# Expert numbers read four at a time, W2 loads in the order of free buffers, and part of the result stored from ScalarE

## What is computed

```python
logits = x2 @ Wr + br
expert = jnp.argmax(softmax(logits), axis=-1)        # one of 8 experts for each node
h   = gelu(einsum('ecd,edf->ecf', buf, W1) + b1)     # W1: 8 x 512 x 128
out = einsum('ecf,efd->ecd', h, W2) + b2             # W2: 8 x 128 x 512
y   = out[slot] * gate
# shared = gelu(x2 @ Ws1 + bs1) @ Ws2 + bs2
# result = x + shared + bank_sp(x) + bank_fq(x)
```

## Time and profile before

| What | Value |
|---|---|
| Runs | 533.3, 534.15, 535.89 us; median 534.15 |
| The profiled execution, time | 538.39 us |
| Its span from first to last instruction | 536.6 us |
| Mean granted TensorE clock | 0.966 |
| PE busy | 476.1 us, 89% of the span |
| DVE, ACT, POOL busy | 224.5, 166.2, 191.8 us |
| SPq's share of the chain that ended last | 11% |

### The profile page before, as it was taken

How to read it: one execution, slowest core, us unless ns; L and a number is a source line. 1 busy time by engine, 2 the same in 40 slices (tenths; PEclk the granted TensorE clock), 3 DMA queues, 4 the chain that set the end, 5 groups by cost and what they waited for, 6 DMA issues and landing times.

```text
span 536.6 us, 7670 instructions
## 1 busy us (share of the span) xinstructions
PE 476.1 (89%) x2638; PEld 328.7 (61%) x2638; DVE 224.5 (42%) x561; ACT 166.2 (31%) x363; POOL 191.8 (36%) x201
## 2 busy tenths in 40 slices
PE   2798999979999997989999999999999999997390
PEld 2344457767566654766677778777877777564050
DVE  4789953213444456432220024300266955353026
ACT  2799663212211117212130133400544232121000
POOL 2103000190502511980537533060362688230072
PEclk9999999989999998999999999999999999999586
DMA  5999999958999789658027001200230037888875
GB/s 120 407 424 420 423 385 347 373 190 296 393 408 414 265 308 413 244 172 333 5 58 217 0 1 4 98 4 1 59 99 0 1 96 220 240 253 243 272 218 167
DMA packets 36597, 115.30 MB, mean 215 GB/s; under 512 B 6495, under 2 KB 6556, under 8 KB 28110
## 3 DMA queue, kind: packets, MB, share of 16 engines
q1 hardware_dynamic: 34318, 112.22, 58.3%
q0 software_dynamic: 2240, 2.57, 1.8%
HBM read 105.76 MB, written 9.01 MB: 214 GB/s over the span
## 4 chain that ended last, share of the span: by engine, by line
PE 64%; SPq 11%; DMA 10%; issue 8%; POOL 3%; DVE 2%; ACT 2%; DVEq 0%; POOLq 0%
PE ps L1494 13%; PE ps L1496 12%; PE ps L1495 12%; PE ps L1853 9%; PE ps L1518 9%; DMA ring<-in_L_gnn_basis_dram 8%; SPq L576 5%; SPq L577 4%; PE ps L1579 2%; PE ps L1698 2%; DMA got<-y_dram,slot_u 1%; PE ps L1502 1%; POOL piece_lo L670 1%; PE ps L1756 1%; ACT h_tmp L1254 1%
## 5 line engine op out<-in xcount | busy, mean ns | idle before, releaser
L1518 PE MATMUL ps<-ring,sel_att 128*32 128x512 f32 x512 | 67.8, 617 | 6.2 <-DMA ring<-in_L_gnn_basis_dram 2.7
L1494 PE MATMUL ps<-piece_hi,ht_hi 128*125 128x512 f32 x140 | 56.1, 401 | 0.8 <-PE ps L1496 0.6
L1495 PE MATMUL ps<-piece_lo,ht_hi 128*125 128x512 f32 x140 | 55.1, 394 | 0.0
L1496 PE MATMUL ps<-piece_hi,ht_lo 128*125 128x512 f32 x140 | 55.1, 394 | 0.0
L1001 DVE SCALAR_TENSOR_TENSOR u_lo<-ps,gates,u_hi 125x512 fp32r<-125x512 f32 x20 | 15.0, 751 | 94.1 <-ACT u_hi L1402 94.1
L669 POOL CAST piece_hi<-piece_raw 128x512 fp32r<-128x512 f32 x28 | 19.9, 710 | 95.1 <-issue 70.7
L670 POOL TENSOR_TENSOR piece_lo<-piece_raw,piece_hi 128x512 fp32r<-128x512 f32 x28 | 37.5, 1339 | 14.4 <-issue 12.3
L851 DVE TENSOR_SCALAR oh_n<-iota_n,keys 125x626 f16<-125x626 f16 x100 | 38.1, 381 | 8.3 <-PE ps L1579 6.2
L1853 PE MATMUL ps<-u_hi,cf 125*125 125x512 f32 x100 | 39.9, 399 | 1.3 <-PE ps L1496 1.3
L1853 PE MATMUL ps<-u_lo,cf 125*125 125x512 f32 x100 | 39.4, 394 | 0.0
L732 POOL TENSOR_SCALAR sort<-iota_s,slot_s 125x864 fp32r<-125x864 f32 x10 | 24.4, 2447 | 32.0 <-PE ps L1941 21.1
(11 more groups left out here) (323 smaller groups left out, 959.9 us busy)
## 6 DMA issues: line engine op xcount, KB each, us to landing
ring<-in_L_gnn_basis_dram SPq DMA_DIRECT2D x64, 1024.0 KB, 9.4
w_home<-in_L_ffn_W_sp_dram SPq DMA_DIRECT2D x27, 256.0 KB, 2.9
w_home<-in_L_ffn_W_fq_dram SPq DMA_DIRECT2D x24, 256.0 KB, 3.1
rel_dram<-stag SPq DMA_DIRECT2D x16, 256.0 KB, 8.4
w_raw<-rel_dram SPq DMA_DIRECT2D x8, 512.0 KB, 6.7
piece_raw<-in_L_mix_Wkqv_dram SPq DMA_DIRECT2D x3, 1024.0 KB, 10.6
y_dram<-ybuf SPq DMA_DIRECT2D x12, 256.0 KB, 3.7
piece_raw<-in_L_mix_W_dram SPq DMA_DIRECT2D x2, 1024.0 KB, 10.8
```

What stands on the lines that cost most here:

```text
L1494: pe.matmul(target, a_hi, b_hi, start=first, stop=False, skip_group_check=skip)
L1495: pe.matmul(target, a_hi, b_lo, start=False, stop=False, skip_group_check=skip)
L1496: return pe.matmul(target, a_lo, b_hi, start=False, stop=last, skip_group_check=skip)
L1518: last = pe.matmul(ps[32 * c:32 * c + 32, rel_bank(ch), :], sel_att[:, ch // CHUNKS, g].rearrange("p r q -> p (r q)"), ring[slot][:, c * D ...
```

## The change

Four edits, all in the last stage.

1. The units are numbered in another order: the last four W1 units of the second bank become 12 to 15, Ws1 becomes 16 and Ws2 17. ACT's and POOL's order follow from that, and POOL's two Ws units no longer stand between its sort tiles.
2. SP begins its W2 loads after unit 12; units 13 to 16 are loaded behind the first three W2 tiles, and unit 17 behind tiles 3 and 13.
3. SP reads the numbers of a tile's blocks with one instruction, four (or three) at a time; tiles are loaded in another order against the stores of finished tiles.
4. Rows 112 to 124 of each result tile are stored from ACT's queue.

```diff
-        UNITS = ([(1, 0, e) for e in range(E)] + [(1, 1, e) for e in range(4)] + [(1, 2, 0), (2, 2, 0)] +
-                 [(1, 1, e) for e in range(4, E)])
+        UNITS = ([(1, 0, e) for e in range(E)] + [(1, 1, e) for e in range(E)] + [(1, 2, 0), (2, 2, 0)])
...
-            for n in range(RAWS, len(UNITS)):
+            for n in range(RAWS, UNIT[1, 1, 4] + 1):
                 load_unit(n)
...
-                for c in range(y_rows(j) // SB):
-                    at = b * NB + 4 * i + c
-                    expert = sp.value_load(block_ei[0:1, at:at + 1], min_val=0, max_val=E - 1)
+                at, count = b * NB + 4 * i, y_rows(j) // SB
+                _, experts = nc.values_load_multi_w_load_instructions(
+                    block_ei[0:1, at:at + count], engines=[mybir.EngineType.SP], min_val=0, max_val=E - 1)
+                for c, expert in enumerate(experts):
                     sp.dma_start(w2_home[HOME[j]][:, c, :], w2_of[b][bass.ds(expert, 1), :, :].rearrange("e f n -> f (e n)")
                                  ).then_inc(w2_in[HOME[j]], 16)
-            for j in (0, 1, 2, 3, 2 * NY - 1):
+            for j in range(3):
                 load_w2(j)
-            for j in range(2 * NY):
-                if j < 3:
-                    load_w2(j + 4)
-                elif j == 3:
-                    for i in range(NY, NY + 3):
-                        load_w2(i)
-                elif j < NY:
-                    load_w2(j + 6)
+            for n in range(UNIT[1, 1, 4] + 1, len(UNITS) - 1):
+                load_unit(n)
+            load_w2(3)
+            load_w2(2 * NY - 1)
+            load_unit(len(UNITS) - 1)
+            load_w2(4)
+            load_w2(5)
+            store_block(0)
+            load_w2(6)
+            store_block(1)
+            for j in range(NY, 2 * NY - 1):
+                load_w2(j)
+                if j > NY:
+                    store_block(j - NY + 1)
+            for j in range(NY, 2 * NY):
                 store_block(j)
             for t in range(NT):
                 sp.wait_ge(final_ready, t + 1)
-                for a, b in ROWS:
-                    sp.dma_start(out[t * TP + a:t * TP + b, :], x1[a:b, t, :]).then_inc(stored, 16)
+                a, b = ROWS[0]
+                sp.dma_start(out[t * TP + a:t * TP + b, :], x1[a:b, t, :]).then_inc(stored, 16)
...
-            unit_rest(UNIT[1, 1, 0], UNIT[1, 2, 0])
+            unit_rest(UNIT[1, 1, 0], UNIT[1, 1, 4])
...
             for t in range(P_TURNS, NT):
                 sort_tile(0, t)
-                unit_rest(UNIT[1, 2, 0] + t - P_TURNS, UNIT[1, 2, 0] + t - P_TURNS + 1)
             unit_rest(UNIT[1, 1, 4], len(UNITS))
...
             shared_row(1)
+            for t in range(NT):
+                act.wait_ge(final_ready, t + 1)
+                a, b = ROWS[1]
+                act.dma_start(out[t * TP + a:t * TP + b, :], x1[a:b, t, :]).then_inc(stored, 16)
```

## The result

The changed kernel takes 526.74 us (median of 4 runs, 526.35 to 527.45) against 535.02 for the one before (4 runs, 533.3 to 537.32): ratio 0.9844, 95% interval 0.9802 to 0.9886. It is 8.3 us faster, half of the 16.7 that was forecast, and the time lies above the range.

The account below looks back on a forecast made before the run. SP's queue of W2 loads and stores was taken to set the last 95 us. Tile 6's store 15.8 us earlier plus 0.9 from the last stores made 16.7: 534.15 - 16.7 = 517.5 us, range 515 to 523.5.

Parts of the forecast that it names:

- The start and the order: SP's loads: first read at 425.8, brief wait before unit 17, about 8 us before tile 4; PE's tile 0 0.94 earlier.
- I take 0.30, since it is one instruction on adjacent words of one row: SP's read of four numbers costs 0.30 us, a group 3.50 instead of 4.40; 40 reads fewer, 12.0 us of SP's work.
- The bounds, one read and four: SP's read of four costs no less than one read, 0.27 us, and not well more than four, 4 x 0.27.
- by the register: Rival: SP's read of four costs by the register, group up to 4.30 us, end 519.5 to 524.4; chance 0.21.
- The 0.6 us that the sum had for reads behind waits: On SP from tile 4 on: a read right after a wait takes up to 0.56 instead of 0.27.
- A store's landing: Tile 6's store, issued at 490.2, lands in about 3.58 us as before, so the first gather starts at 494.1.
- the DMA engines become the bound: Rival: late W2 loads and stores need 329 GB/s against 302, nine rounds 3.2 us longer, end 520.7; chance 0.12.
- The other chain: PE's second-bank tiles end at 496.1, 16.6 us earlier; the second gather keeps its distance to the first.
- ACT's work on Ws2: Rounding Ws1 and Ws2 costs ACT about 1.1 us more, hidden in 3.79 us of idle time; put at nothing.
- The range checks: On SP, 0.27 us per block kept; if cheap within a group, SP gains up to 3 us, about 1.2 arriving.
- the stall for unit 17: Rival: SP waits long for POOL's low half before unit 17, end 545, 11 us later than now; slower, chance 0.03.
- a gain lost behind POOL: Rival: gain lost behind PE or POOL, only 0.94 and 0.9 us remain, end about 532; chance 0.04.

Follow-up runs that it names:

- the probes: The changed kernel with range-checked idle reads of varied start and count added on SP, in its wait before tile 4 and behind five stores; 536.38 us including them.
- Experiments 2 and 3: 2: the changed kernel with one read per block again, 529.22 us. 3: the kernel before with the grouped reads alone, old order and stores, 529.41 us.
- the aligned kernel: The changed kernel with one word of padding, so the second bank's numbers start at word 28 instead of 27; 519.38 us, again side by side 521.04.
- 7: The kernel with padded numbers, reading four words for the two tiles of three blocks too (fourth unused, DVE clears the row first); 521.01 us, repeated 522.14.

## Why the prediction was wrong

**The start and the order were right.** SP's first load stands 2.1 us after `block_ei` (0.2 for the write, then the read and eight checks of the whole group), the wait for unit 17 is 1.3 us and harmless, SP stands 8.4 us ahead of tile 4 (about 8 forecast), the 0.94 of idle time before PE's first sort is gone, and PE's tile 0 starts 452.18 - 423.52 = 28.7 us after `block_ei`; before, 455.41 - 425.57 = 29.8.

**The step that failed is "I take 0.30, since it is one instruction on adjacent words of one row".** It is right for the six groups of four of the first bank and wrong for the six of the second, which stand in the stretch that sets the end, and for both groups of three. The bounds, one read and four, had the 0.87 of a word-by-word read inside them, and the rival "by the register" named it; what neither had is that the price depends on the start address, and that such a read can grow to 1.65 us, beyond the upper bound of 1.07. So the 526.7 lies above that rival's 524.4 too. Tiles 7 to 12 cost 7.7 us in reads instead of 1.8, tile 6 0.4 more: together 6.3 us. Tile 6's store is 6.0 us later than in the sum, counted from `block_ei` (494.13 - 423.52 = 70.6 instead of 490.2 - 425.57 = 64.6). With one word of padding it is at 489.64 - 424.72 = 64.9. The 0.6 us that the sum had for reads behind waits rests on a wrong reading of the earlier trace rows: the 0.56 stands 1.58 us behind a store, and in the changed kernel the reads of tiles 4 and 5, behind waits for PE, took 0.30 and 0.29.

The sentence on the Trainium skill's rule ("Runtime: NRT & Kernel Launch", section "Instruction fetch mechanics", about 200 ns for each register even in bulk) comes out as follows: 0.20 for each further word is what the probes show for every read but the aligned four, and there the rule doesn't hold.

**A store's landing was mis-sized:** 3.58 taken, 4.96 measured, which makes the gather start another 1.4 us later. The sum took the time of a store behind evenly spaced loads and used it for one behind four loads in a burst. Experiments 2 and 3 show that the grouping goes with it and the mean traffic doesn't. An estimate from rows gives about half of the size: four loads, 1.0 MB, issued within 2.0 us, against engines that moved at most 379 to 400 GB/s here, leave about 0.3 MB ahead of the store, some 0.7 us. Where the rest comes from is open. The rival "the DMA engines become the bound" had its ceiling at 302 GB/s, which is wrong, since 379 were moved; in the changed kernel it didn't come (share 0.80), in the aligned one it begins (0.97).

**The rest:** from the first gather to the end of DVE's adds it took 499.43 to 521.06 = 21.6 us, 0.45 less than before; the last stores brought 0.7 in the profile (0.9 forecast), which the runs can't show. Sum: 6.0 + 1.4 - 0.45 + 0.2 = 7.2 us, what was to be found in the stage.

**The other chain** was forecast too early as well, without harm. PE ended its tiles 78.7 us after `block_ei` (502.26), where the sum had 496.1 - 425.57 = 70.5. It waited for loads which SP issued late, and behind the first wait the granted clock was 0.50 (1.2 GHz) from 494.41 to 504.65, and 1.00 (2.4 GHz) until then: tile 12 took 1.94 us and tile 13 1.93, where the sum had 0.96 and 0.72 at full clock (columns as in the earlier trace rows). The earlier trace rows already had 1.93 for tile 13 before. POOL then waited 0.92 us for the second bank's stores, where it had waited 0.77 before. ACT's work on Ws2, which the sum put at nothing, cost nothing: ACT waited 2.67 us for Ws2 and PE's tile 0 did not wait. That hangs on the grouped reads, since with single ones (experiment 2) PE waited 1.0.

```profile
494.50:504.60 10.10, 5.97 (x23) 2.99 (x24) 1.82 (x4) 0.60 (x1) 4.26 (x4) 0.50 0.90 269
```

**The range checks** stayed near their full price in a group, 0.15 + 0.02 with their gaps, 0.26 for each number (1.02 for four, 491.04 to 492.06, instead of 1.08); the reservation that they could get cheap was not needed. Without them the first gather starts 5.8 us sooner, counted from `block_ei` (64.3 instead of 70.1 in 7), and the runs show nothing of it.

**The other rivals:** the stall for unit 17 and a gain lost behind POOL did not come. With the reads as forecast, in the aligned kernel, the stage is 96.4 us where the forecast had 111.0 - 16.7 = 94.3. What lacks there is the landing of the stores: tile 6's is issued within 0.3 us of the forecast, and the gather starts 6.2 us behind it instead of 3.9.

**Left open:** what it is in a store's issue that lengthens a read 1 to 2 us later, and whether an aligned four is spared because it is one piece or because it was nearly always over by then. The one that wasn't took 0.44. An experiment that puts aligned fours 1.6 us behind the stores would tell; none was made.

## What to carry to other kernels

When one instruction takes the place of several, its price is not between one and four by guess: measure it at each address and count that the loop will use, above all at those where the second half of a table begins. A queue that only issues (SP here) can be the bound of a stage, so count its reads, checks and issues like arithmetic. And where an edit bunches transfers that were evenly spaced, count on the one at the end of the bunch to land later: part of the queue's gain is paid back there.

## What was not expected of the hardware

- SP reads four words into registers in 0.30 us if the first stands at a multiple of four words, and in 0.87 if not; one word costs 0.27, two 0.47, three 0.67, at the starts tried (0 and 1, for two words 2 as well). Reading three costs more than reading four.
- A read that was still at work 1 to 2 us after the issue of a store mostly took longer: fours word by word up to 1.85 us, single reads up to 0.74, the one aligned four 0.44. Loads in flight alone did nothing to it: 0.87 with the engines at 349 GB/s.
- A 256 KB store behind four loads in 1.9 us lands in 4.9 to 5.0 us (median), behind the same loads at 1.1 us each in 3.7 to 3.9, at nearly the same mean rate (251 and 247 GB/s).
- The DMA engines moved 251 GB/s at a busy share of 0.80, and 379 at 0.99: busy share and rate don't rise in proportion.
